# Two graph layers on one core: neighbour sums placed between the experts' chunks, two reloads moved into the join, and TensorE's signals raised by drains

## The reference

```python
# layer 0, feed-forward: a graph attention makes the gates of four experts
h = (x_flat @ W_gat).reshape(M, 4, 4)
e = leaky_relu(a_src[src] + a_dst[dst], 0.2)
ee = exp(e - segment_max(e, dst)[dst])
agg = segment_sum(h[src] * (ee / segment_sum(ee, dst)[dst]), dst) + b_gat
w = softmax(top_k(layernorm(agg).mean(heads), 2))
for ei in range(4):
    out += g[ei] * (gelu(x @ W1[ei] + b1[ei]) @ W2[ei] + b2[ei])   # 256 -> 512 -> 256
# layer 1, mixer: linear attention over nodes, then relu(x @ W1 + b1) @ W2 + b2 (256 -> 1024 -> 256)
out = einsum('blhd,bhde,blh->blhe', q_phi, kv, z).reshape(..., 256) @ Wo + bo
```

## Time and profile before

| | before |
|---|---|
| median of 3 runs | 4406.01 us (4398.67 to 4411.37) |
| profiled execution | 4400.95 us, its span 4399.2 us |
| `gat_edges` up to the experts' end | 1014.6 to 2053.6 us |
| sort of layer 1's edges | 2100.4 to 2404.6 us |
| mixer loop of layer 1 | 2736 to 3577 us |
| last stage (`Ffn1`) | 3662 to 4399 us |

### The profile page before, as it was taken

The page is one execution under the profiler, slowest core; times in us unless marked ns, Lnnn a source line. Parts: engine busy times, 40 slices in busy tenths (PEclk is TensorE's granted clock), DMA queues, the critical chain, the costliest instruction groups (busy, mean ns, idle before and its releaser), DMA issues. The chain is left out here.

```text
span 4399.2 us, 45890 instructions
## 1 busy us (share of the span) xinstructions
PE 2388.0 (54%) x14500; PEld 1769.9 (40%) x14500; DVE 1799.8 (41%) x3887; ACT 1362.5 (31%) x3051; POOL 1277.8 (29%) x1238
## 2 busy tenths in 40 slices
PE   3677455634111110896475126434535466899997
PEld 2532324533000110664352125333434354688885
DVE  6898355770000000113899674434434366111112
ACT  2479235631000000111268001434434332122221
POOL 0000040005777776000000215545344421500005
PEclk9999676765555555998599568667767676999998
DMA  1210112003111111111130213434333320354553
GB/s 62 93 37 0 46 32 79 0 1 60 22 13 12 9 11 11 34 33 41 60 118 39 74 36 78 156 98 149 112 126 136 97 89 21 107 188 188 186 188 93
DMA packets 165531, 322.54 MB, mean 73 GB/s; under 512 B 71298, under 2 KB 126592, under 8 KB 156845
## 3 DMA queue, kind: packets, MB, share of 16 engines
q0 software_dynamic: 62656, 149.60, 12.2%
q1 hardware_dynamic: 102753, 171.54, 11.5%
HBM read 213.40 MB, written 107.37 MB: 73 GB/s over the span
## 5 line engine op out<-in xcount | busy, mean ns | idle before, releaser
L1645 POOL DMA_INDIRECT ge_near<-gat_src,s_other x512 | 516.4, 1009 | 171.9 <-issue 171.9
L1947 PE MATMUL bank<-arena 128*125 128x256 f32 x800 | 219.9, 438 | 627.6 <-issue 582.8
L2752 POOL DMA_INDIRECT he_buf<-wh_dram,s_other x400 | 387.0, 967 | 404.3 <-DVEq L2986 283.5
L1947 PEld LDWEIGHTS bank<-arena 128*125 128x125 f32 x800 | 170.5, 218 | 683.9 <-issue 622.5
L1974 DVE TENSOR_TENSOR XN<-bank,arena 125x256 f32 (+1 forms) x100 | 42.4, 425 | 984.2 <-remote 580.1
L1960 ACT ACTIVATE arena<-bank,arena 128x500 f32<-128x500 f32 (+1 forms) x112 | 70.6, 633 | 957.8 <-DMA q_gb<-in_L_mix_bn_beta_cols 657.7
L2872 ACT ACTIVATE he_buf<-he_buf,he_e 128x128 f32<-128x128 f32 x800 | 239.4, 387 | 36.8 <-issue 34.4
L2432 ACT ACTIVATE x_hT<-bank,x_w 128x256 f32<-128x256 f32 x256 | 121.4, 474 | 379.4 <-PE bank L2384 379.4
L2393 PE MATMUL bank<-x_w,x_hT 128*128 128x256 f32 x1024 | 229.4, 382 | 6.9 <-ACT x_hT L2432 6.7
L2384 PE MATMUL bank<-x_xT,x_w 128*128 128x256 f32 x1024 | 228.1, 381 | 0.9 <-DVE x_xT L2187 0.9
L2393 PEld LDWEIGHTS bank<-x_w,x_hT 128*128 128x128 f32 x1024 | 191.9, 190 | 39.3 <-issue 13.2
(11 more groups left out here) (696 smaller groups left out, 5989.9 us busy)
## 6 DMA issues: line engine op xcount, KB each, us to landing
he_result<-he_buf SPq DMA_DIRECT2D x25, 2080.0 KB
XN<-s_a_dram SPq DMA_DIRECT2D x57, 512.0 KB
x_y<-XN SPq DMA_DIRECT2D x24, 500.0 KB
x_x<-zero SPq DMA_DIRECT2D x1, 8192.0 KB, 27.0
ge_near<-gat_src,s_other POOLq DMA_INDIRECT x512
x_xs<-x_x SPq DMA_DIRECT2D x32, 256.0 KB, 3.4
x_y<-x_ys SPq DMA_DIRECT2D x32, 256.0 KB, 2.1
he_buf<-wh_dram,s_other POOLq DMA_INDIRECT x400
```

What stands on the lines that cost most here:

```text
L1645: pool.indirect_dma_start(out=G[:, c, 0:HF + H], out_offset=None, in_=m.gat_src, in_offset=bass.IndirectOffsetOnAxis(ap=ed.other[:, c:c + ...
L1947: last = pe.matmul(m.ps[4 + j % 2][:P, 0:D], self.hT[:, f, j * P:(j + 1) * P], w.w2[e][:, f, :], start=f == 0, stop=f == FC - 1)
L2752: pool.indirect_dma_start(out=buf[j][:, c, 0:HF + H], out_offset=None, in_=m.wh_dram, in_offset=bass.IndirectOffsetOnAxis(ap=ed.other[:, t ...
```

## The change

**Sort.** The 32 scans of `vector_scan` have a drain after every fourth, instead of one at the end.

**Edge sums of layer 0.** The quarters become parts of 128, 64, 192 and 128 columns. `logits` is split into `scores` and `maxima`, `sums` into `weigh` and `sums` for some heads. `s.spread` stands before expert 2. Part 0 stands between the chunks of expert 2 and part 1 between those of expert 3, on DVE, with ACT's two exponentials after chunk 1; the loops of these two experts are written out. Parts 2 and 3 stand after the sort, in another order. `dec` has one buffer instead of two.

**Reloads.** The reload of expert 3's result (before: SP, right after the sort) and that of expert 0's (before: its own block) stand on SP inside `join_nodes`, after its last gather has landed; the block is gone.

**Signals.** In `Experts0.tensor` and in the mixer of layer 1 each of PE's counters is raised by a drain behind the group, instead of by the group's last matmul: 8 drains a full chunk in the experts (4 `up`, 4 `down`), about 15 an iteration in the mixer.

```diff
         for i in range(KB):
             dve.tensor_tensor_scan(H3[:, 1:, i], m.ones[:, 0:self.cols], H3[:, 1:, i], start[:, i:i + 1],
                                    ALU.mult, ALU.add)
-        dve.drain()
+            if i % 4 == 3:
+                dve.drain()
...
+
+            if then is not None:
+                @block.sync
+                def _(sp):
+                    sp.wait_ge(rows[NG - 1], 16 * GT)
+                    then(sp)
...
+            PARTS = ((0, 128), (128, 192), (192, 384), (384, 512))
+            dec = m.sb("ge_dec", [128, 192, H])
+            dec_of = lambda q: dec[:, 0:PARTS[q][1] - PARTS[q][0], :]
...
                     sp.wait_ge(s1.negated, 1)
                     ex.reload(sp, 1)
                     ex.reload(sp, 2)
-                    sp.wait_ge(sorted1, 1)
-                    ex.reload(sp, 3)
                     keep(2)
                     keep(3)
...
 
-                    def logits(q):
-                        lo, hi = q * CQ, (q + 1) * CQ
+                    def scores(q):
+                        lo, hi = PARTS[q]
                         e = spread.ke[:, lo:hi, :]
+                        blocks_done = hi // BC
                         for j in range(2):
-                            dve.wait_ge(rows[j], 16 * BC * (hi // BC // 2))
+                            dve.wait_ge(rows[j], 16 * BC * ((blocks_done + 1 - j) // 2))
                         dve.tensor_tensor(e, G[:, lo:hi, HF:HF + H], e, ALU.add)
                         dve.drain()
                         dve.scalar_tensor_tensor(e, e, 0.2, e, ALU.mult, ALU.max)
                         dve.drain()
+
+                    def maxima(q):
+                        lo, hi = PARTS[q]
+                        e, d = spread.ke[:, lo:hi, :], dec_of(q)
                         for h in range(H):
                             dve.tensor_tensor_scan(mx[:, lo:hi, h], spread.pen[:, lo:hi], e[:, :, h],
                                                    mx[:, lo - 1, h:h + 1] if q else -BIG, ALU.add, ALU.max)
                         dve.drain()
-                        d = dec[:, q % 2 * CQ:(q % 2 + 1) * CQ, :]
                         if q == 0:
                             dve.memset(d[:, 0, :], 0.0)
                         first = 1 if q == 0 else 0
@@ -1678,44 +1688,64 @@
                                           ALU.subtract)
                         dve.tensor_tensor(e, e, mx[:, lo:hi, :], ALU.subtract)
                         dve.drain()
-                        wide = spread.cont[:, lo:hi].unsqueeze(2).broadcast_to((128, CQ, H))
+                        wide = spread.cont[:, lo:hi].unsqueeze(2).broadcast_to((128, hi - lo, H))
                         dve.tensor_tensor(d, d, wide, ALU.mult)
                         dve.drain().then_inc(e_ready, 1)
 
-                    def sums(q):
-                        lo, hi = q * CQ, (q + 1) * CQ
-                        e, d = spread.ke[:, lo:hi, :], dec[:, q % 2 * CQ:(q % 2 + 1) * CQ, :]
+                    def weigh(q):
+                        lo, hi = PARTS[q]
+                        e, d = spread.ke[:, lo:hi, :], dec_of(q)
                         dve.wait_ge(e_exp, q + 1)
-                        dve.tensor_tensor(d, d, spread.cont[:, lo:hi].unsqueeze(2).broadcast_to((128, CQ, H)), ALU.mult)
+                        dve.tensor_tensor(d, d, spread.cont[:, lo:hi].unsqueeze(2).broadcast_to((128, hi - lo, H)), ALU.mult)
                         for h in range(H):
                             f = G[:, lo:hi, h * F:(h + 1) * F]
-                            dve.tensor_tensor(f, f, e[:, :, h].unsqueeze(2).broadcast_to((128, CQ, F)), ALU.mult)
+                            dve.tensor_tensor(f, f, e[:, :, h].unsqueeze(2).broadcast_to((128, hi - lo, F)), ALU.mult)
                         dve.drain()
-                        for h in range(H):
+
+                    def sums(q, heads):
+                        lo, hi = PARTS[q]
+                        e, d = spread.ke[:, lo:hi, :], dec_of(q)
+                        for h in heads:
                             for f in (*range(h * F, (h + 1) * F), HF + h):
                                 dve.tensor_tensor_scan(G[:, lo:hi, f], d[:, :, h], G[:, lo:hi, f] if f < HF else e[:, :, h],
                                                        G[:, lo - 1, f:f + 1] if q else 0.0, ALU.mult, ALU.add)
-                        dve.drain().then_inc(summed, 1)
+                        if H - 1 in heads:
+                            dve.drain().then_inc(summed, 1)
+
+                    def beside(q):
+                        def between(dve, c):
+                            if c == 0:
+                                scores(q)
+                            elif c == 1:
+                                maxima(q)
+                            elif c == 2:
+                                weigh(q)
+                            elif c == 3:
+                                sums(q, (0, 1))
+                            elif c == 4:
+                                sums(q, (2, 3))
...
                     s.positions(dve)
-                    for e in range(4):
-                        ex.vector(dve, e)
+                    ex.vector(dve, 0)
+                    ex.vector(dve, 1)
                     s.spread(dve)
                     dve.drain()
-                    logits(0)
-                    logits(1)
-                    sums(0)
-                    sums(1)
+                    ex.vector(dve, 2, beside(0))
+                    ex.vector(dve, 3, beside(1))
                     dve.wait_ge(ex.freed, 4 * (NCH + 1))
                     s1.vector(dve)
-                    dve.drain().then_inc(sorted1, 1)
-                    logits(2)
-                    logits(3)
-                    sums(2)
-                    sums(3)
+                    scores(2)
+                    maxima(2)
+                    scores(3)
+                    weigh(2)
+                    sums(2, range(H))
+                    maxima(3)
+                    weigh(3)
+                    sums(3, range(H))
...
                     def weights(q):
-                        lo, hi = q * CQ, (q + 1) * CQ
+                        lo, hi = PARTS[q]
                         act.wait_ge(e_ready, q + 1)
                         act.activation(spread.ke[:, lo:hi, :], spread.ke[:, lo:hi, :], ACT.Exp)
-                        d = dec[:, q % 2 * CQ:(q % 2 + 1) * CQ, :]
-                        act.activation(d, d, ACT.Exp)
+                        act.activation(dec_of(q), dec_of(q), ACT.Exp)
                         act.drain().then_inc(e_exp, 1)
-                    for e in range(4):
-                        ex.scalar(act, e)
-                    weights(0)
-                    weights(1)
+
+                    def beside(q):
+                        def between(act, c):
+                            if c == 1:
+                                weights(q)
+                        return between
+                    ex.scalar(act, 0)
+                    ex.scalar(act, 1)
+                    ex.scalar(act, 2, beside(0))
+                    ex.scalar(act, 3, beside(1))
                     s1.scalar(act)
                     weights(2)
                     weights(3)
...
-            @block.sync
-            def _(sp):
-                sp.wait_ge(r_stored, 64)
-                ex.reload(sp, 0)
+        def reload(sp):
+            ex.reload(sp, 3)
+            ex.reload(sp, 0)
         join_nodes(m, "gj", ed, spread, H, F, NT, last, result, (r_stored, 64), add_nodes, own_e,
                    Arena(spread.ke[:, :, :].rearrange("p t h -> p (t h)"), cols * H).take,
-                   Arena(near[:, NT * D:], cols * W - NT * D).take)
+                   Arena(near[:, NT * D:], cols * W - NT * D).take, reload)
 
...
             for f in range(FC):
                 pe.wait_ge(self.acted, c * FC + (e * (NCH + 1) * FC + f + 1))
                 for k in range(K2):
-                    last = pe.matmul(m.ps[f % 4][:, 0:nt * P], w.w1[e][:, k, f * 128:(f + 1) * 128],
+                    pe.matmul(m.ps[f % 4][:, 0:nt * P], w.w1[e][:, k, f * 128:(f + 1) * 128],
                                      m.XT[:, bass.ds(c * CH + k * N, nt * P)], start=k == 0, stop=k == K2 - 1)
-                last.then_inc(self.up, 1)
+                pe.drain().then_inc(self.up, 1)
             pe.wait_ge(self.acted, c * FC + (e * (NCH + 1) * FC + FC + 4))
             for j in range(nt):
                 pe.wait_ge(self.kept, c * 4 + (e * NT + j + (2 if j == 0 else 1)))
                 for f in range(FC):
-                    last = pe.matmul(m.ps[4 + j % 2][:P, 0:D], self.hT[:, f, j * P:(j + 1) * P], w.w2[e][:, f, :],
+                    pe.matmul(m.ps[4 + j % 2][:P, 0:D], self.hT[:, f, j * P:(j + 1) * P], w.w2[e][:, f, :],
                                      start=f == 0, stop=f == FC - 1)
-                last.then_inc(self.down, 1)
+                pe.drain().then_inc(self.down, 1)
         chunks(pe, body)
 
...
```

(34 more changed lines are left out.)

29 lines of the change are left out of this document (14 added, 15 removed).

## The result

The changed kernel took 4443.36 us (median of 5 runs, 4431.8 to 4504.24), the kernel before 4405.95 us (5 runs, 4398.67 to 4411.37): ratio 1.0097, 95% interval 1.0075 to 1.0118. It is slower by 1%, where 3805 had been forecast. The profiled execution took 4443.36 us, its span 4441.7, against 4400.95 and 4399.2.

The account below looks back on a forecast made before the run. It held late PE signals beside POOL's gathers to bound the experts, with the mixer alike. 4401 - 487 (through the sort) + 12 (after it) - 125 (mixer) = 3801, forecast 3805; range 3640 to 4460, its own case 3600 to 4050.

Parts of the forecast that it names:

- does a drain's increment escape the lateness?: Experts and mixer: whether PE drains signal promptly beside gathers, where matmul signals come 2.80 us a record; yes given 0.52.
- the first side: PE beside gathers: drains signal promptly, since an engine emptied every 4 or 8 records might never fall behind.
- term 1: Experts: with prompt drains a chunk takes 17.1 us, 25 chunks 428, ending near 1469 instead of 2053.6.
- the two signs of being wrong: Experts: PE drains of 11 us behind `up` groups and 22 behind a tile's; additions still 22.4 us apart.
- term 3: Sort: starting from 1484 beside the remaining gathers at half pace, it ends at 1918 instead of 2404.8, -487 us.
- ACT's 11.64 us around a drain: Mixer, trace before: ACT held around its drain of line 2868, cited for both sides, as sitting out the backlog and recovering.
- The experts' price: Experts: each PE drain exposes 0.3 us at a group's end, bounds 0.1 and 0.6, 8 drains a chunk.
- the slower rival: Experts and mixer: drains wait like everything else, sum +52, 4458 us (4405 to 4520); chance 0.23.
- The hidden edge work: Between experts and sort: spread and quarters 0 and 1 hidden, sort starting 15 instead of 46.8 us after the experts, -32.
- The work after the sort: Edge sums after the sort: 320 columns instead of 256, +8.8, and about 2 for an exposed exponential.
- The reloads: Join: two reloads of 3.2 MB with 30 us of cover, 0 or +8, taken as +4.
- The mixer: Mixer of layer 1: prompt signals take 10 of 67 us off each of 12.5 iterations, -125 (0 to -340).

Follow-up runs that it names:

- f2: Kernel before, POOL waiting after every eighth gather of layer 0 until these have landed: 4016.62 us, ratio 0.9172.
- h1: Kernel before, POOL waiting after every fourth gather of layer 0 until these have landed: 4029.56 us, ratio 0.9143.
- e4: Kernel before with both reloads behind the join's gathers and the block between the stages gone: 3466.08 us, ratio 1.0102.
- e1: Kernel before with PE's counters raised by drains in the mixer of layer 1 alone: 3443.89 us, ratio 1.0035.
- i1: Kernel before with waits after every eighth gather in layer 0 and mixer, edge sums between expert chunks, and mixer drains: 3803.05 us, ratio 0.8689.
- f3: Changed kernel without the mixer's drains: 4470.27 us, ratio 1.0209 to the kernel before.
- f1: Changed kernel once more, unaltered: median 4470.66 us beside 4377.09 for the kernel before.
- f4: Kernel before with edge sums between the chunks and the mixer's drains: median 4356.71 us, ratio 0.9876 without its four longest runs.
- i2: Kernel before with drains in the four experts of layer 0 alone: 4461.06 us, ratio 1.0175.
- h4: Kernel before with waits after every eighth gather in layer 0 and mixer, and edge sums between chunks of experts 2 and 3: 3806.06 us, ratio 0.865.
- h2: Kernel before with waits after every eighth gather in layer 0 and in the mixer's stage: 3822.52 us, ratio 0.8685.
- g2: Kernel before with a memset and a drain on POOL after each gather of layer 0: 4545.85 us, ratio 1.3242.
- h3: Kernel before with a memset on POOL after each gather of layer 0, with its own counter and no drain: 4316.89 us, ratio 0.9797.

## Why the prediction was wrong

**The step that failed** is the one that decides, "does a drain's increment escape the lateness?", answered with the first side, and with it term 1 of the sum. In the experts a PE drain beside gathers lasts 22.30 us behind a tile and 11 behind an `up` group, the two signs of being wrong that the prediction names, and the additions stay 22.40 apart. With term 1 (experts at 1469, measured 2132.2) the -487 of term 3 went. The argument taken was that PE's matmuls are on time and only what follows their completion is not; but the rows show only when matmuls start, and their ends are modelled. The row that pointed the other way was ACT's 11.64 us around a drain, and it was the right one to go by. The Trainium skill (PSUM — Partial Sum Buffer, on engine and sequencer instructions) says that a drain waits for the engine to go fully idle. The 22.30 us agree, and by that sentence a drain signals no earlier than the matmuls in front of it are complete.

**Why the evidence for it misled.** That an earlier stage signals promptly beside gathers was true, and it only showed that the lateness has a condition. The experts' own start shows the same. In the trace of before, 18 gathers had started when ACT's third Gelu of expert 0 came on time, and the fourth was late:

```profile
1038.59 0.68 ACT L1960 ACTIVATE arena<-bank,arena 128x500 f32<-128x500 f32 x1 [1.00 <-issue]
...
1045.39 0.68 ACT L1960 ACTIVATE arena<-bank,arena 128x500 f32<-128x500 f32 x1 [6.12 <-DMA q_gb<-in_L_mix_bn_beta_cols]
```

The third Gelu still came 1.68 us behind the second, the fourth 6.80 behind the third. f2 and h1 show a condition that the code can reach: POOL's gathers in long rows without a wait. Emptying PE after every 4 or 8 records, which the prediction counted on, changes nothing in the experts beside the gathers. Where the signals are prompt, the rest of the forecast was near: f2's experts end at 1429, its sort beside the gathers takes 544 us, which term 3 had between 304 and 564 with 434 as its choice.

**The experts' price.** 0.3 us a drain was 0.445: 3.56 us a chunk, the experts' end +78.6 with ACT's exponentials, where the slower rival had +48 and +9.

**The hidden edge work.** -32 in that rival, measured -33.8. The work after the sort +7.6 against +10.8, the sort's drains +1.5 against 2, the join -1.8 against -5: right in kind and nearly in size.

**The reloads.** +4 was +36. The term asked whether 30 us cover the reloads' own users and left out what stands behind them on SP's queue, the gates' three parameter loads. e4 has this term alone, +35.

**The mixer.** Forecast -125 by prompt signals, in the slower rival +15; measured -56.9 in the profiled execution. PE's drains there are late too: those of line 2888 (`down`) last 10.85 us in the median, those of the same place 3.84 in e1, without lateness, and 3.84 in i1, with pauses. Between f3 and f1 the loop shows 43 us, between f2 and f4 only 4. Why the drains seem to help there and not in the experts is not settled. In the traces of the changed kernel and of f1 nearly all gathers fall into rows of 16 with breaks between, in those without drains into rows of 32, and in f4, where the gain is missing, a part is rows of 32 again. As breaks are what helped in f2, this may be the way, but it was only seen, not tested. What the drains are worth in the median is open.

**The slower rival** had the mechanism, and 4458 (4405 to 4520) for it. It came near by errors that cancel: experts 22 too little, the gates' loads 32 too little, the mixer 72 too much. Its chance of 0.23 was too low for what the earlier trace rows showed.

**Shown and not shown.** Shown: drains don't hasten the experts' signals (i2, the drains' record); the parameter loads' wait (e4); waits between gathers take 8% off where completions are late, 13% in both stages. Not shown: what differs between the groups, and by what path gathers hold up completions of PE. PE, ACT and DVE all fall to the same 1.40 us an instruction (for PE, half of 2.80 a record), so it may be something that the engines share, but no run tells what. Every execution here also had its instructions recorded, for its span and clock, so no run tells either whether the recording has a part in it.

## What to carry to other kernels

Before changing how a late signal is raised, find what runs beside it and break that up: eight gathers and a wait took 360 us away where a drain took nothing. When a transfer is moved, list what is issued behind it on its queue, down to the smallest load. Time a kernel on more than one occasion, always beside the kernel before; the pauses that save 13% where completions are late cost 7% where they are not.

## What the runs showed of the hardware

The same program on the same chip takes 3431 us in one group and 4404 in another. In the groups with late completions, PE's completions beside a long row of indirect gathers come 2.80 us for each matmul record (22.40 us for a tile's 8), which as a weight load and a matmul would be 1.40 us each; ACT's fall to 1.40 us an instruction. With a wait after every fourth gather the experts keep PE's pace (end at 1421, h1), with one after every eighth mostly (1429 in f2, 1461 in h4, 1580 in h2). A drain on PE behind a dense group costs 0.445 us (18.28 against 14.72 a chunk). A memset and a drain on POOL behind an indirect DMA hold the next one up, gathers 3 to 7 us apart instead of 1.25 (g2); with the memset alone they are 1.28 apart (h3).
